# Turning only the maxima's parts, and norming rows a batch sooner

## The chip, the cores and the metric

One core of a Trainium2 chip. PE is TensorE, DVE is VectorE, ACT is ScalarE, POOL is GpSimd, and SP issues most transfers. The metric is the device time of one execution in microseconds; a kernel is told by the median of its runs.

## The reference, cut to what matters

```python
h = _L0_tok_ref(x, ...)                    # 8 x 1024 x 64
h = jnp.concatenate([h, txt], axis=1)      # 8 x 1056 x 64
h = h + _L0_attn_ref(_layernorm(h, axis=-1), qkv_w, qkv_b, proj_w, proj_b, rpb_table)
h = h + _L0_ffn_ref(_layernorm(h, axis=-1), ...)
h = h + _L1_attn_ref(_layernorm(h, axis=-1), ...)
h = h + _L1_ffn_ref(_layernorm(h, axis=-1), ...)
# _L0_attn_ref: 8 heads of 8, 1056 rows
attn = jnp.einsum('bnhd,bmhd->bhnm', q * scale, k)
attn = jax.nn.softmax(attn + bias[None], axis=-1)
out = jnp.einsum('bhnm,bmhd->bnhd', attn, v)
```

The change touches the layer norm ahead of the first attention, and the first attention's scores.

## The kernel before, in words

The kernel is a row of stages, each with its own code on each engine; between stages results go through DRAM, and a stage's buffers lie beside those of its neighbours. The order of work on every engine is written out by hand, with semaphores between them. Two stages are touched.

**heads_prep** ("the preparation", tiles `pre_...`) goes over 8 batches of 1056 rows, 9 tiles of 128 rows. DVE measures mean and variance (`measure`, L717 to L725), POOL takes the root (`root`, L784), DVE norms the rows (`norm`, L730). PE turns the normed rows (`turn`, L824), ACT copies them out (`copy_turned`, L872), PE multiplies them by the query, key and value weights (L831). Each number is then written as a sum of three bf16 parts into rows of 64 slots for each head, queries into `qs` and keys into `ks`: ACT writes the high part three times (L886), DVE forms the rest (L960), POOL writes the queries' middle part (L804) and ACT the keys' (L905), DVE the low part (`low`, L944). Slots 0 to 2 of every head stay empty in the queries and hold ones in the keys. PE turns `qs` and `ks` to 64 slots by rows (L849, 8 groups of 8, through three PSUM banks, and L856 for the last 32 rows), DVE copies the turned queries out (L969, tails L973), ACT the turned keys (L910). SP stores values, the stacked queries `qs` (`qs_d`, L762), turned queries (`qt_d`, L767) and turned keys (`kt_d`, L769). In batch b DVE begins with `measure` and `norm` of batch b + 1, then makes the rests and low parts of b. ACT begins b + 1's high parts only when the store of b's `qs` has landed (`qs_out`). In batch 3, SP issues the next stage's first loads (`ahead`); after batches 4 to 6 DVE makes a part of the next stage's corner (`early`, L1455 to L1465).

**attend_heads** ("the first attention", tiles `att_...`) goes over 32 pairs of heads, one after the other. For the next pair, PE computes all scores once in bf16 (L1531 and others, 37 pieces in three PSUM banks) and DVE takes their maxima over the keys (L1711, L1713, L1716). DVE writes the negated maxima, again as three bf16 parts, into slots 0 to 2 of the stacked queries `qs` that were loaded from `qs_d` (L1723 to L1730); PE turns the whole of `qs` (`turn`, L1552 and L1554), and ACT copies the result to `qm` (`turned`, L1651 and L1654). The scores of the pair are then key times `qm` (L1592, L1595), so that the maxima are subtracted by the matmul; ACT takes the exponential (L1679), and PE multiplies by the values (L1624). The maxima are computed from `qT`, which was loaded from `qt_d` and has empty slots 0 to 2.

What PE does beside each of the 27 pieces of a pair's scores is in one list, in which the turn stands between the third and the fourth maximum of the pair after the next:

```python
AHEAD, BETWEEN = 9, 3
side = ([("max", 1, m) for m in range(AHEAD, NM)] + [("max", 2, m) for m in range(BETWEEN)]
        + [("turn", 1, w) for w in range(QT)] + [("max", 2, m) for m in range(BETWEEN, AHEAD)])
```

Each entry takes the next of three banks (`ring_free`): PE waits until DVE has reduced, or the turned queries have been copied out of, what stood in it three entries earlier. PE waits for both turned parts (`t_cp`) ahead of a pair's first scores.

Of the kernel before, what the change touches and what calls it, by code (L numbers as in the profile page):

```python
# [24 lines left out]
P = 128  # L25
# [620 lines left out]
def heads_prep(nc, a, const, ps, h_in, qt_d, kt_d, qs_d, v_d, vt_d):  # L646
# [9 lines left out]
    with ExitStack() as ctx:  # L656
# [21 lines left out]
         tail_cp, vt_made, q_out, k_out, vt_out, qs_out) = nm.sems(  # L678
            "w_in", "w_scaled", "zeroed", "ones_set", "t_in", "t_split", "consts_set", "st_made", "agg_made",
            "var_made", "tail_set", "half_set", "rstd_made", "xn_made", "xt_mm", "xt_cp", "qkv_mm", "hi_made", "rest_made",  # L680
            "qmid_made", "kmid_made", "low_made", "qt_mm", "qt_cp", "kt_cp", "tail_cp", "vt_made", "q_out", "k_out", "vt_out",
            "qs_out")
# [17 lines left out]
        def ready(sp, b):  # L700
            for x in (q_out, k_out, vt_out, qs_out):
                sp.wait_ge(x, 16 * (b + 1))
            sp.wait_ge(v_out[b % 2], 16 * (b // 2 + 1))
# [42 lines left out]
        def _(sp):  # L746
            enter(sp, const, "sp")
            first_loads(sp, const)

            def step(b, par, more):  # L750
# [20 lines left out]
            two_ahead(sp, step)  # L771

        @block.gpsimd
        def _(pool):
# [20 lines left out]
            tidy(pool, const)  # L795
            for b in range(0, B):
                if b + 1 < B:
                    root(b + 1)
                for m in range(NB):
# [5 lines left out]
                        .then_inc(qmid_made, 1)  # L805
                pool.wait_ge(qmid_made, (b + 1) * NB)
# [57 lines left out]
        def _(act):  # L864
            enter(act, const, "act")
            act.wait_ge(ones_set, 5)
            def copy_turned(b):
                at_least(act, qkv_mm, b * NB)
                for c in range(3):
# [46 lines left out]
        def _(dve):  # L916
# [61 lines left out]
            by_two(dve, step)  # L978
# [372 lines left out]
def attend_heads(nc, a, const, ps, qt_d, kt_d, qs_d, v_d, vt_d, o_d, corner):  # L1351
# [30 lines left out]
    with ExitStack() as ctx:  # L1382
        nm = Names(nc, ctx, const, stage)
        qT = nm.sb("qT", [P, U, N], BF16)
        qm = nm.sb("qm", [P, 2, N], BF16)
        qs = nm.sb("qs", [P, U, NT, P], BF16)
# [14 lines left out]
        (set_up, mrow_set, t_in, cor_rest, cor_hi, s_mm, p_made, pv_mm, o_cp, mx_mm, mx_red, m_row, m_hi, m_r1, m_mid,  # L1401
         c_made, t_mm, t_cp) = nm.sems(
            "set_up", "mrow_set", "t_in", "cor_rest", "cor_hi", "s_mm", "p_made", "pv_mm", "o_cp", "mx_mm", "mx_red", "m_row",
# [4 lines left out]
        NL = 16 * 9  # L1408
# [18 lines left out]
        def load(sp, it, u):  # L1427
# [80 lines left out]
        def _(pe):  # L1508
# [38 lines left out]
            def turn(w, u, pos):  # L1547

                bank = ps[:, 4 + pos % MRING, :].bitcast(BF16)
                if w == 0:  # L1550
                    for t in range(FULL):
                        mm = pe.transpose(bank[:, t * P:(t + 1) * P], qs[:, u, t, :], eye[:, :])  # L1552
                else:
                    mm = pe.transpose(bank[:, 0:2 * TT], qs[0:2 * TT, u, FULL, :], eye[0:2 * TT, 0:2 * TT])  # L1554
# [26 lines left out]
            def scores(it, u, g, last):  # L1581
# [3 lines left out]
                for c, (_, i) in enumerate(parts):  # L1585
# [5 lines left out]
                    if i is None:  # L1591
                        mm = pe.matmul(ps[0:2 * TT, bank, 0:TH], kz[:, u, :], qm[:, u % 2, cols], start=True, stop=not near)  # L1592
# [51 lines left out]
        def _(act):  # L1644
            enter(act, const, "act")
            def turned(k, u, w):

                bank = ps[:, 4 + side.index(("turn", 1, w)) % MRING, :].bitcast(BF16)
                act.wait_ge(t_mm, k * QT + w + 1)
                if w == 0:  # L1650
                    cp = act.activation(qm[:, u % 2, 0:TX], bank[:, :], ACT.Identity)  # L1651
                else:
                    for s in range(2):
                        cp = act.activation(qm[half(s), u % 2, TX:N], bank[half(s), s * TT:(s + 1) * TT], ACT.Identity)  # L1654
                cp.then_inc(t_cp, 1)

            def step(it, last):
# [7 lines left out]
                for u in range(U):  # L1665
                    for g, (t, parts) in enumerate(groups):
                        for c, (_, i) in enumerate(parts):
# [13 lines left out]
                            if not (last and u == U - 1):  # L1681
                                for w in range(QT):
                                    if cut[n % NU] <= side.index(("turn", 1, w)) < cut[n % NU + 1]:
                                        turned(it * U + u + 1, (u + 1) % U, w)
# [7 lines left out]
            for w in range(QT):  # L1692
                turned(0, 0, w)
# [2241 lines left out]
```

## Time and profile before

| | us |
|---|---|
| median of 3 runs | 2805.91 |
| lowest and highest | 2793.22, 2813.04 |
| the profiled execution | 2807.24 |
| its span, first to last instruction | 2805.4 |
| PE, DVE, ACT, POOL busy | 2508.5, 1976.2, 1523.8, 400.7 |
| moved by transfers | 174.09 MB |

The profile comes from one execution. Busy time is the time in which an engine had an instruction under way; an idle time is put down to what ended it. The granted clock is given in tenths of full speed, where 1.00 is 2.4 GHz and 0.50 is 1.2 GHz. Times in the rows count from the first instruction.

### The profile page before, as it was taken

Reading aid. Unit: us, or ns where it says so; the run is one execution under the profiler, and the core shown is the slowest. Engines: PE = TensorE matmul, PEld = TensorE weight load, DVE = VectorE, ACT = ScalarE, POOL = GpSimd, SP = SyncE. Lnnn points to the kernel's source line nnn. Section 1 sums busy time; section 2 is a strip of 40 time slices with the busy share of each in tenths; the row PEclk is TensorE's granted clock in tenths of the full one; section 3 lists DMA queues with packets and bytes.
Section 4 is the critical chain, followed back from the end, with each engine's and each line's share of the span. In section 5 each row is a group of like instructions: output and inputs, shape, how many; then the busy total and the mean of one; then the engine's idle time right before and its main releaser. Section 6 shows DMA issues by size and latency. Waiting matters only on the chain. (4 is left out here: it accounts for less than half of the span.)

```text
span 2805.4 us, 52471 instructions
## 1 busy us (share of the span) xinstructions
PE 2508.5 (89%) x18409; PEld 1100.5 (39%) x18456; DVE 1976.2 (70%) x5061; ACT 1523.8 (54%) x2639; POOL 400.7 (14%) x500
## 2 busy tenths in 40 slices
PE   7877558999999999998699998997679999699999
PEld 3223542333333333333433333565544444433333
DVE  6776668888888888883477776557676765366665
ACT  4323653777777777775244443325656667143443
POOL 1110210000000000003311112122100101411110
PEclk9998667999999999998699999655689999599999
DMA  2001751111111111122500001234441223701100
GB/s 84 16 16 47 252 206 43 33 48 33 48 48 33 49 39 42 48 53 48 108 18 18 18 15 28 56 83 127 156 141 62 82 62 66 149 12 31 31 21 15
DMA packets 272054, 174.09 MB, mean 62 GB/s; under 512 B 225121, under 2 KB 230050, under 8 KB 270546
## 3 DMA queue, kind: packets, MB, share of 16 engines
q1 hardware_dynamic: 258626, 142.45, 18.9%
q0 software_dynamic: 10368, 19.06, 2.2%
q10 hardware_dynamic: 2808, 9.22, 1.5%
q8 instruction: 158, 2.59, 0.4%
q14 instruction: 94, 0.77, 0.1%
HBM read 96.19 MB, written 74.53 MB: 61 GB/s over the span
## 5 line engine op out<-in xcount | busy, mean ns | idle before, releaser
L1711 DVE TENSOR_REDUCE att_mpart<-ps 128x1 f32<-128x512 f32 x1024 | 635.4, 683 | 82.5 <-PE ps L1531 52.5
L1679 ACT ACTIVATE att_p<-ps 128x704 f32<-128x704 f32 x768 | 543.6, 760 | 136.1 <-PE ps L1595 131.4
L1624 PE MATMUL ps<-att_p,att_v 128*9 128x352 f32 x3072 | 300.5, 462 | 0.1
L1531 PE MATMUL ps<-att_kT,att_qT 64*128 64x512 bf16 x1024 | 276.4, 386 | 20.8 <-DMA att_qz<-qt_d 8.5
L1595 PE MATMUL ps<-att_qm,att_kT 64*128 64x352 bf16 x1536 | 251.8, 317 | 10.5 <-ACT att_p L1679 8.2
L1325 DVE TENSOR_REDUCE cau_mpart<-ps 128x1 f32<-128x512 f32 (+5 forms) x384 | 193.0, 551 | 81.2 <-PE ps L1151 68.0
L2462 ACT ACTIVATE mo_act<-ps,mo_b 128x768 f32<-128x768 f32 x176 | 156.3, 901 | 132.2 <-PE ps L2344 128.7
L2615 DVE TENSOR_TENSOR mo_g<-mo_act,ps 128x768 f32<-128x768 f32 x176 | 167.3, 951 | 77.3 <-PE ps L2379 41.2
L1292 ACT ACTIVATE cau_p<-ps 128x704 f32<-128x704 f32 (+6 forms) x272 | 171.6, 660 | 82.3 <-PE ps L1210 49.6
L3014 ACT ACTIVATE mo_act<-ps 128x1024 f32<-128x1024 f32 (+1 forms) x108 | 102.9, 953 | 194.1 <-PE ps L2928 193.9
L1595 PEld LDWEIGHTS ps<-att_qm,att_kT 64*128 64x128 bf16 x1536 | 82.8, 93 | 287.6 <-issue 278.1
L1502 POOL DMA_DIRECT2D o_d<-att_o x128 | 64.1, 507 | 846.0 <-ACT att_o L1662 845.9
L2344 PE MATMUL ps<-mo_x,mo_wf 64*128 64x384 f32 x704 | 162.9, 540 | 0.9 <-issue 0.9
L3125 DVE TENSOR_TENSOR mo_g<-mo_act,ps 128x1024 f32<-128x1024 f32 (+1 forms) x108 | 122.1, 1130 | 50.1 <-PE ps L2940 47.3
L2396 PE MATMUL ps<-mo_g,mo_w 128*64 128x384 f32 x704 | 151.8, 510 | 0.4 <-DVE mo_g L2615 0.4
L1210 PE MATMUL ps<-cau_qT,cau_kT 128*128 128x352 bf16 (+7 forms) x576 | 128.5, 287 | 1.8 <-ACT cau_p L1292 1.5
L1531 PEld LDWEIGHTS ps<-att_kT,att_qT 64*128 64x128 bf16 x1024 | 85.0, 94 | 88.3 <-issue 54.0
L1148 PE MATMUL ps<-cau_kT,cau_qT 128*128 128x384 bf16 (+5 forms) x353 | 105.4, 331 | 14.6 <-ACT cau_qT L1267 7.7
L2940 PE MATMUL ps<-mo_gx,mo_w 64*128 64x512 f32 (+3 forms) x576 | 112.8, 592 | 0.2 <-DVE mo_g L3125 0.2
L600 DVE TENSOR_TENSOR mix_g<-ps,mix_gamT 128x512 f32<-128x512 f32 x128 | 86.1, 686 | 33.2 <-PE ps L404 32.7
L2952 PE MATMUL ps<-mo_g,mo_w 128*64 128x512 f32 (+1 forms) x432 | 108.8, 582 | 0.4 <-DVE mo_g L3125 0.2
L2928 PE MATMUL ps<-mo_x,mo_w 64*128 64x512 f32 (+1 forms) x432 | 108.8, 581 | 0.0
(446 smaller groups left out, 4271.7 us busy)
## 6 DMA issues: line engine op xcount, KB each, us to landing
qs_d<-pre_qs SPq DMA_DIRECT2D x8, 1152.0 KB, 4.5
att_qs<-qs_d SPq DMA_DIRECT2D x32, 288.0 KB, 4.1
qt_d<-pre_qT SPq DMA_DIRECT2D x8, 1056.0 KB, 4.4
kt_d<-pre_kT SPq DMA_DIRECT2D x8, 1056.0 KB, 7.4
att_kT<-kt_d SPq DMA_DIRECT2D x32, 264.0 KB, 2.8
att_qT<-qt_d SPq DMA_DIRECT2D x32, 264.0 KB, 3.1
cqt_d<-cpr_qT SPq DMA_DIRECT2D x8, 1056.0 KB
cau_qT<-cqt_d SPq DMA_DIRECT2D x16, 528.0 KB, 4.0
```

The lines of the kernel that those rows point to most:

```text
L1210: mm = pe.matmul(ps[r0:r0 + kn, at, off:TH], kT[:, u, tile * P:tile * P + kn], qT[:, u, s, q], start=True, stop=m1 <= m0)
L1292: e = act.activation(p[:, n % RING, :, off:TH], ps[:, bank:bank + 2, off:TH], ACT.Exp)
L1325: red = dve.tensor_reduce(mpart[:, j, s, i:i + 1], ps[:, 4 + place, 0:w], AX.X, ALU.max)
L1531: mm = pe.matmul(ps[:, bank, :], qT[half(s), u, j * P:(j + 1) * P], kT[half(s), u, c * BANK:(c + 1) * BANK], start=True, stop=not near)
L1595: mm = pe.matmul(ps[:, bank + s, 0:TH], kT[half(s), u, i * P:(i + 1) * P], qm[half(s), u % 2, cols], start=True, stop=not near)
L1624: mm = pe.matmul(ps[32 * cg:32 * cg + DV, 7, 0:TH], v[:, u, i, s, :], p[:, r, s, :], start=i < 2, stop=i == FULL - 1)
L1679: e = act.activation(p[:, n % PRING, :, :], ps[:, bank:bank + 2, 0:TH], ACT.Exp)
L1711: red = dve.tensor_reduce(mpart[:, j, s, c:c + 1], ps[:, bank, :], AX.X, ALU.max)
L2344: mm = pe.matmul(ps[0:m, bank + s, 0:EN], wf[s * C:(s + 1) * C, w0 + n * P:w0 + n * P + m], x1[s * C:(s + 1) * C, par, :], start=True, sto ...
L2396: mm = pe.matmul(ps[s * C:(s + 1) * C, ACC, 0:EN], w2[0:m, n, :], g[0:m, (par * NH + n) % RING, s, :], start=n == 0 and not relu, stop=n = ...
L2462: act.activation(act1[0:m, r, :, :], ps[0:m, zb:zb + 2, 0:EN], ACT.Relu, bias=b1[0:m, n:n + 1])\
L2615: dve.tensor_tensor(g[0:m, r, :, :], src[0:m, r, :, :], ps[0:m, bank:bank + 2, 0:EN], ALU.mult)\
```

## The change

In the preparation, `qs` is no longer stored, and nobody waits for that store. `measure` and `norm` run a batch sooner: in batch b DVE begins with `measure` of b + 2, and `norm` of b + 2 comes after the fourth copy of turned queries; `root` of b + 2 comes after POOL's middle parts; SP loads the rows of b + 3 in batch b; measure and norm of batch 1 stand ahead of the loop. ACT's three copies of the next batch's turned rows stand between its middle parts instead of before them.

In the first attention, `qs` is neither loaded nor kept. A tile `mz` of two buffers, cleared once by POOL, takes the maxima's parts only; PE turns it as it turned `qs`, and DVE adds the result to the turned queries `qT` in place, behind the first three maxima of the next pair. The scores read `qT` in place of `qm`.

```diff
 # heads_prep, sync: the loads and stores
+            sp.wait_ge(xn_made, NT)
+            load(sp, 2, 0)
...
-                if more:
-                    sp.wait_ge(xn_made, (b + 1) * NT)
-                    load(sp, b + 2, par)
+                if b + 3 < B:
+                    sp.wait_ge(xn_made, (b + 2) * NT)
+                    load(sp, b + 3, 1 - par)
...
-                sp.wait_ge(low_made, (b + 1) * 2 * NB)
-                sp.dma_start(qs_d[bass.ds(b, 1)].rearrange("b p n -> (b p) n"), qs[:, :, :].rearrange("p t n -> p (t n)"))\
-                    .then_inc(qs_out, 16)
 # gpsimd
+            root(1)
             for b in range(0, B):
-                if b + 1 < B:
-                    root(b + 1)
...
+                if b + 2 < B:
+                    root(b + 2)
 # scalar
-                at_least(act, qs_out, b * 16)
...
-                if not last:
-                    copy_turned(b + 1)
                 for m in range(NB):
                     n = tiles(m)
+                    if not last and 1 <= m < 4:
+                        copy_turned(b + 1, (m - 1,))
 # vector
-                if not last:
-                    measure(dve, b + 1, 1 - par)
-                    norm(dve, b + 1, 1 - par)
+                if b + 2 < B:
+                    measure(dve, b + 2, par)
...
                     dve.tensor_copy(qT[:, u, 0:TX], ps[:, (2 * u) % 3, :].bitcast(BF16)).then_inc(qt_cp, 1)
+                    if u == 3 and b + 2 < B:
+                        norm(dve, b + 2, par)
...
+            measure(dve, 1, 1)
+            norm(dve, 1, 1)
 # attend_heads
-        qm = nm.sb("qm", [P, 2, N], BF16)
-        qs = nm.sb("qs", [P, U, NT, P], BF16)
+        mz = nm.sb("mz", [P, 2, NT, P], BF16)
...
-                             (qs[:, u, :, :], qs_d[bi].rearrange("b p (t n) -> (b p) t n", t=NT)[:, :, u * P:(u + 1) * P]),
...
+            pool.memset(mz[:, :, :, :], 0.0).then_inc(mz_set, 1)
...
-                        mm = pe.transpose(bank[:, t * P:(t + 1) * P], qs[:, u, t, :], eye[:, :])
+                        mm = pe.transpose(bank[:, t * P:(t + 1) * P], mz[:, u, t, :], eye[:, :])
...
-                            mm = pe.matmul(ps[:, bank + s, 0:TH], kT[half(s), u, i * P:(i + 1) * P], qm[half(s), u % 2, cols],
+                            mm = pe.matmul(ps[:, bank + s, 0:TH], kT[half(s), u, i * P:(i + 1) * P], qT[half(s), u, cols],
...
+            def turned(k):
+                u = k % U
+                for w in range(QT):
+                    bank = ps[:, 4 + side.index(("turn", 1, w)) % MRING, :].bitcast(BF16)
+                    dve.wait_ge(t_mm, k * QT + w + 1)
+                    if w == 0:
+                        add = dve.tensor_tensor(qT[:, u, 0:TX], qT[:, u, 0:TX], bank[:, :], ALU.add)
+                    else:
+                        for s in range(2):
+                            add = dve.tensor_tensor(qT[half(s), u, TX:N], qT[half(s), u, TX:N],
+                                                    bank[half(s), s * TT:(s + 1) * TT], ALU.add)
+                    add.then_inc(t_cp, 1)
...
                 for m, (kind, s, j, c) in enumerate(maxes):
+                    if m == BETWEEN and k > 0:
+                        turned(k - 1)
```

ACT's `turned`, which copied to `qm`, goes.

## Rows read from the trace of the kernel before

**Rows 1.** Windows: us, then busy us (count) of PE, PEld, DVE, ACT, POOL; PEclk, DMA, GB/s.

```profile
260.00:415.00 155.00, 93.61 (x792) 82.98 (x792) 97.50 (x417) 98.07 (x336) 28.31 (x49) 0.68 0.60 209
456.00:1310.00 854.00, 836.01 (x7684) 285.62 (x7682) 711.66 (x1357) 650.64 (x1052) 62.10 (x124) 1.00 0.16 41
856.00:883.00 27.00, 26.69 (x252) 9.13 (x251) 23.38 (x45) 20.73 (x36) 2.00 (x4) 1.00 0.17 43
```

**Rows 2.** Waits within ten pairs, 600 to 866.3 us: sum, times, longest.

```profile
ACT att_p L1679 <- PE ps L1595: 40.8, 60, 1.3
```

**Rows 3.** Order of time, DVE, around the turn of one pair: start, us.

```profile
800.07 1.88 DVE L1711 TENSOR_REDUCE att_mpart<-ps 128x1 f32<-128x512 f32 x3
802.77 0.69 DVE L1711 TENSOR_REDUCE att_mpart<-ps 128x1 f32<-128x512 f32 x1 [0.83 <-PE ps L1535]
803.95 9.89 DVE L1711 TENSOR_REDUCE att_mpart<-ps 128x1 f32<-128x512 f32 x16 [0.48 <-PE ps L1531]
```

**Rows 4.** Order of time, ACT, the same stretch.

```profile
802.67 0.39 ACT L1654 ACTIVATE att_qm<-ps 64x32 bf16<-64x32 bf16 x2
```

**Rows 5.** Order of time, PE, the same stretch.

```profile
801.55 0.20 PE L1554 MATMUL ps<-eye,att_qs 64*128 64x64 bf16 x1
...
803.54 0.38 PE L1531 MATMUL ps<-att_kT,att_qT 64*128 64x512 bf16 x2
```

**Rows 6.** Order of time, PE, in the preparation, parts of several batches.

```profile
281.81 3.19 PE L831 MATMUL ps<-pre_w,pre_xT 65*128 65x192 f32 x18
...
287.04 2.10 PE L824 MATMUL ps<-eye,pre_xn 128*64 128x128 f32 x9 [2.04 <-DVE pre_xn L730]
...
292.57 1.01 PE L849 MATMUL ps<-eye,pre_qs 128*128 128x128 bf16 x8 [3.43 <-DVE pre_ks L944]
...
333.38 3.19 PE L831 MATMUL ps<-pre_w,pre_xT 65*128 65x192 f32 x18
...
355.97 3.19 PE L831 MATMUL ps<-pre_w,pre_xT 65*128 65x192 f32 x18
...
375.12 3.19 PE L831 MATMUL ps<-pre_w,pre_xT 65*128 65x192 f32 x18
...
395.43 3.19 PE L831 MATMUL ps<-pre_w,pre_xT 65*128 65x192 f32 x18
...
404.40 1.03 PE L849 MATMUL ps<-eye,pre_qs 128*128 128x128 bf16 x8 [5.78 <-DVE pre_ks L944]
...
411.01 0.25 PE L856 MATMUL ps<-eye,pre_ks 32*128 32x32 bf16 x4
```

**Rows 7.** Order of time, DVE, in the preparation, batches 4 and 6.

```profile
336.44 1.24 DVE L717 BATCH_NORM_STATS2 pre_bst<-pre_h 128x6 f32<-128x64 f32 x9 [2.59 <-DMA pre_h<-hidden]
...
379.27 1.23 DVE L717 BATCH_NORM_STATS2 pre_bst<-pre_h 128x6 f32<-128x64 f32 x9
...
383.54 2.10 DVE L730 TENSOR_SCALAR pre_xn<-pre_h,pre_stats,pre_rstd 128x64 f32<-128x64 f32 x9 [1.99 <-POOL pre_rstd L784]
```

**Rows 8.** Order of time, ACT, in the preparation, batches 1, 4 and 7.

```profile
288.34 1.38 ACT L872 ACTIVATE pre_xT<-ps 64x512 f32<-64x512 f32 x3
...
340.23 0.33 ACT L886 ACTIVATE pre_qs<-ps 128x192 bf16<-128x192 f32 x1 [6.29 <-DMA qs_d<-pre_qs]
...
401.95 1.53 ACT L905 ACTIVATE pre_ks<-pre_rest 128x256 bf16<-128x256 f32 x5
```

**Rows 9.** Page, transfers: KB each, us from issue to landing.

```profile
att_qs<-qs_d SPq DMA_DIRECT2D x32, 288.0 KB, 4.1
```

**Rows 10.** Groups by line and form, DVE: busy, mean ns, idle before.

```profile
L1711 DVE TENSOR_REDUCE att_mpart<-ps 128x1 f32<-128x512 f32 x1024 | 635.4, 683 | 82.5 <-PE ps L1531 52.5 <-PE ps L1535 28.4
...
L3125 DVE TENSOR_TENSOR mo_g<-mo_act,ps 128x1024 f32<-128x1024 f32 x96 | 117.0, 1219 | 45.6 <-PE ps L2940 42.8 <-issue 2.2
...
L969 DVE COPY pre_qT<-ps 128x1024 bf16<-128x1024 bf16 x32 | 22.1, 692 | 28.3 <-PE ps L849 28.3
...
L973 DVE COPY pre_qT<-ps 128x128 bf16<-128x128 bf16 x8 | 1.8, 225 | 1.9 <-PE ps L856 1.8
```

More of the change, by code:

```diff
@@ L643, in ln_scale, with heads_prep @@
     dve.reciprocal(rstd[:, 0:n], sq[:, 0:n]).then_inc(rstd_made, 1)
[L646 removed]
+def heads_prep(nc, a, const, ps, h_in, qt_d, kt_d, v_d, vt_d):
     H, D = 8, 8
@@ L700, in ready @@
         def ready(sp, b):
-            for x in (q_out, k_out, vt_out, qs_out):
+            for x in (q_out, k_out, vt_out):
                 sp.wait_ge(x, 16 * (b + 1))
@@ L748, in _, with step @@
             first_loads(sp, const)
-            def step(b, par, more):
+            sp.wait_ge(xn_made, NT)
+            load(sp, 2, 0)
+            def step(b, par):
                 if b == 3:
                     ahead(sp, const)
-                if more:
-                    sp.wait_ge(xn_made, (b + 1) * NT)
-                    load(sp, b + 2, par)
+                if b + 3 < B:
+                    sp.wait_ge(xn_made, (b + 2) * NT)
+                    load(sp, b + 3, 1 - par)
                 sp.wait_ge(hi_made, (b + 1) * NB)
@@ L769, in step @@
                 sp.dma_start(kt_d[bass.ds(b, 1)].rearrange("b u p n -> p (b u) n"), kT[:, :, :]).then_inc(k_out, 16)
-            two_ahead(sp, step)
+            for b in range(B):
+                step(b, b % 2)
         @block.gpsimd
@@ L866, in _, with copy_turned @@
             act.wait_ge(ones_set, 5)
-            def copy_turned(b):
+            def copy_turned(b, chunks=range(3)):
                 at_least(act, qkv_mm, b * NB)
-                for c in range(3):
+                for c in chunks:
                     n = min(4, NT - 4 * c) * P
@@ L976, in step @@
                     early(dve, const, "dve", b - 3)
-            by_two(dve, step)
+            measure(dve, 1, 1)
+            norm(dve, 1, 1)
+            for b in range(B):
+                step(b, b % 2, b == 0, b == B - 1)
         yield ready
@@ L1348, in attend_causal, with attend_heads @@
         yield ready
-def attend_heads(nc, a, const, ps, qt_d, kt_d, qs_d, v_d, vt_d, o_d, corner):
+def attend_heads(nc, a, const, ps, qt_d, kt_d, v_d, vt_d, o_d, corner):
     stage = "att"
@@ L1407, in attend_heads @@
         block = const["block"]
-        NL = 16 * 9
+        NL = 16 * 8
         def half(s):
@@ L1547, in turn @@
             def turn(w, u, pos):
+                u = u % 2
                 bank = ps[:, 4 + pos % MRING, :].bitcast(BF16)
@@ L1551, in turn @@
                     for t in range(FULL):
-                        mm = pe.transpose(bank[:, t * P:(t + 1) * P], qs[:, u, t, :], eye[:, :])
+                        mm = pe.transpose(bank[:, t * P:(t + 1) * P], mz[:, u, t, :], eye[:, :])
                 else:
-                    mm = pe.transpose(bank[:, 0:2 * TT], qs[0:2 * TT, u, FULL, :], eye[0:2 * TT, 0:2 * TT])
+                    mm = pe.transpose(bank[:, 0:2 * TT], mz[0:2 * TT, u, FULL, :], eye[0:2 * TT, 0:2 * TT])
                 mm.then_inc(t_mm, 1)
@@ L1591, in scores @@
                     if i is None:
-                        mm = pe.matmul(ps[0:2 * TT, bank, 0:TH], kz[:, u, :], qm[:, u % 2, cols], start=True, stop=not near)
+                        mm = pe.matmul(ps[0:2 * TT, bank, 0:TH], kz[:, u, :], qT[:, u, cols], start=True, stop=not near)
                     else:
                         for s in range(2):
-                            mm = pe.matmul(ps[:, bank + s, 0:TH], kT[half(s), u, i * P:(i + 1) * P], qm[half(s), u % 2, cols],
+                            mm = pe.matmul(ps[:, bank + s, 0:TH], kT[half(s), u, i * P:(i + 1) * P], qT[half(s), u, cols],
                                            start=True, stop=not near)
@@ L1645, in _ @@
             enter(act, const, "act")
[L1646 to L1655, printed above, removed]
             def step(it, last):
@@ L1680, in step @@
                             e.then_inc(p_made, 1)
[L1681 to L1684, printed above, removed]
                         if pending is not None:
@@ L1690, in step @@
                 out_third(*pending)
-            for w in range(QT):
-                turned(0, 0, w)
             body(act, step)
@@ L1733, in step @@
                 for u in range(U - 1 if last else U):
-                    make(it * U + u + 1, (u + 1) % U)
-            make(0, 0)
+                    make(it * U + u + 1)
+            make(0)
             body(dve, step)
+            turned(IT * U - 1)
         yield ready
@@ L3881, in program @@
             token_mix(nc, a, const, ps, hid[0]),
-            heads_prep(nc, a, const, ps, hid[0], qt_d, kt_d, qs_d, v_d, vt_d),
-            attend_heads(nc, a, const, ps, qt_d, kt_d, qs_d, v_d, vt_d, o_d, a["corner"]),
+            heads_prep(nc, a, const, ps, hid[0], qt_d, kt_d, v_d, vt_d),
+            attend_heads(nc, a, const, ps, qt_d, kt_d, v_d, vt_d, o_d, a["corner"]),
             project(nc, a, const, ps, "prj", 8, 8, o_d, a["L0_attn_proj_w"], a["L0_attn_proj_b"], hid[0], hid[1]),
```

15 lines of the change are left out of this document (7 added, 8 removed).

## The prediction

> **What bounds the kernel now.** I read the windows of the two stages first, then the waits inside each, then the order of time on each engine.
>
> The first attention (456 to 1310 us) holds PE for 836.01 of 854 us at granted clock 1.00, DVE for 711.66 and ACT for 650.64; one of the 32 pairs of heads takes 26.7 us, and in 27 us PE is busy 26.69, DVE 23.38, ACT 20.73 [rows 1]. ACT's largest wait is for PE's scores, 40.8 us in ten pairs [rows 2]. So PE is the bound of the pairs, DVE has 3.2 us to spare in each, and what ACT gets back is worth nothing there.
>
> The preparation (260 to 415 us) has no full engine: PE 93.61, DVE 97.50, ACT 98.07 of 155 us, granted clock 0.68, DMA 0.60 [rows 1]. It is a chain. The batches' first query/key/value matmuls start at 281.81, ..., 333.38, 355.97, 375.12, 395.43, and the last transposes end at 411.26 [rows 6]. A batch is ACT writing the high parts, DVE the rests and the low parts, then PE turning 8 groups while DVE and ACT copy out; PE's bank reuse ties it to these, and the next batch's first matmul follows. What a batch costs is the front (first matmul to first transpose) and the turning. The front is 10.76 us in batch 1 and 8.97 in batch 7, which has no norm ahead of it; the turning 6.46 and 6.86 [rows 6].
>
> **The change, part by part.**
>
> (a) Preparation, norm moved. Before, DVE starts a batch with measure (2.28 us), waits 1.99 for POOL's root, norms in 2.1, and only then makes the rests [rows 7]. After, measure stands there alone, the root is made while DVE works on, and norm comes behind the fourth query copy. The norm is then between that copy and the tail copies: these, and the stores of turned queries and keys queued on SP behind them, come 2.1 us later. PE needs the tail's bank only after 3.2 us of matmuls, so that is covered. Measure alone ends some 4.5 us into the batch (0 at the first matmul, 2.1 norm less 0.2, 0.3 tails, 2.3 measure), while ACT is still writing high parts until 6.52 (401.95 less 395.43 [rows 6, 8]); DVE catches up. The end of the front is then ACT's: 6.52, plus five middle parts 1.53 [rows 8], plus the three copies of the next batch's turned rows, 1.38 [rows 8], which now stand between them, plus one low part and the handover, 0.3: 9.6 us with overlaps. Turning: PE sits still from 5.3 (3.19 matmuls, 2.10 turning of rows [rows 6], now back to back) to 9.6, a gap of 4.3 where it was 3.43 (turning 6.46) and where 5.78 gave 6.86 [rows 6]: I take 6.5.
> - Batches 1 to 3: 51.57 us before (333.38 less 281.81 [rows 6]); 3 x 16.1 = 48.3 after: 3.3 saved. Batch 0, where PE at half clock sets the front: 0.3.
> - Batch 5: the queue on DVE holds a part of the next stage's corner, measure, wait, norm; the wait of 1.99 goes, nothing else. The gap before turning grows to 6.3, turning by some 1.2: 0.7 saved.
> - Batch 6: nothing is left to measure. Wait and measure go, 4.27 us, the gap costs 0.95 back: 3.3 saved.
> - Batch 7 had no norm: 0.
>
> (b) Preparation, stacked queries not stored. ACT waited for that store once, 6.29 us, in batch 4, whose length is 22.59 us against 17.2 of its neighbours [rows 6, 8]; there SP issues the next stage's first loads, and everything behind them (the rows of a later batch, whose landing DVE awaited 2.59 us until 336.44) is late [rows 7]. Two stacked-query loads of ten loads go from that list of SP, but the list starts 2.1 later because the tail copies do, and I take the two as nearly even, 0.2 later. The rows landed 3.1 us into batch 4 (336.44 less 333.38); with batch 3 shorter by 0.9, those for batch 6's measure land 4.2 us into it, measure ends at 6.5, and rests and low parts take 4.1 more (in batch 1 from the norm's end, some 1.5 us after PE's 287.04, to 292.57 [rows 6]): 10.6; turning 6.8 after a long gap: 17.4. Saved 5.2. In the other batches nobody waited for this store, and I count it at nothing.
>
> Sum of the preparation: 3.3 + 0.3 + 0.7 + 3.3 + 5.2 = 12.8 us.
>
> (c) First attention. 32 loads of 288 KB go [rows 9]; PE never waits for them, DMA is at 0.16: nothing. ACT loses its turned copies, which ended at 803.06 in the pair shown [rows 4]. DVE gains, behind the first three maxima of the next pair, one addition over 1024 columns and two over 32. The transposes are there at 801.75 [rows 5], DVE reaches them at 801.95 and now sits idle 0.83 and 0.48 us on either side of the fourth maximum, 1.31 us together [rows 3]. The trace has no addition of two bf16 tensors. Its nearest row by type, source and columns is the copy of 1024 bf16 out of PSUM, 692 ns; the addition with the same columns in f32 takes 1219 ns [rows 10]. The two narrow ones together I take at 0.25, a tail copy's 225 ns and a bit [rows 10]. I take the copy's price, since the type halves it: a maximum over 512 f32 columns of PSUM takes 683 ns, the copy of 1024 bf16 692 [rows 10]. 0.69 + 0.25 = 0.94, inside 1.31. The new wait for the transposes has the fourth maximum and all behind it queued on DVE; PE waits for those through its ring of three banks, and for the additions before it refills the two turned banks and before the next pair's first scores. Then the banks are free at 802.95, earlier than ACT's 803.06, and PE asks for them at 803.54 [rows 4, 5]: 0 per pair. With 1.22 + 0.25 = 1.47 they are free at 803.45: still before 803.54, and DVE is 0.16 late: at most 0.2 x 31 = 6 us. Below nothing: PE pauses 0.3 us in 27 [rows 1], so 31 pairs can't give more than some 5 us, and those pauses are not at the turn.
>
> The Trainium skill speaks on both sides of that price. "VectorE: DVE Perf Modes", section "What auto-detection actually checks", has two elements a cycle for an instruction whose tensors are all 16-bit with unit step, two-source ones included; that would be 0.69. Section "Mode 1× (REGULAR) — the baseline" of the same page counts operands in PSUM among what falls back to one element a cycle; that would be 1.22. The rows of the copy agree with the first for one source; no row has two.
>
> (d) Edges. POOL clears the new tile, 2304 columns, after its last middle part; it has the whole last turning for it, 404.40 to 411.26 [rows 6], before DVE comes to the stage: nothing; were it longer, it would cost its excess once. At the stage's first pair the additions stand where ACT copied: 0 to 0.3 us.
>
> **The sum.** The profiled execution took 2807.24 us, span 2805.4 and 1.8 around it. 2807.2 - 12.8 = 2794.4; the median of the runs shown, 2805.91, is 1.3 lower, so 2793.1: 2793.
>
> **The rivals.**
> 1. Slower: the hole is no hole. DVE idles 0.48 us before the fifth maximum because PE's next maxima stand behind a group of values; if the addition costs 1.22 and PE's order just shifts with it, only the 0.83 is filled, and 1.47 - 0.83 = 0.64 us is added to each of 31 pairs: 20 us, 2813, which is above 2806. It decides once additions and hand-overs pass 1.31 us; below 0.94 it is out. For it: DVE runs 16 maxima without a pause behind this place, at 0.617 each, so a delay is not made good soon, and PE's three banks leave it 0.2 us of room. Against: DVE has another 2 us idle later in the pair, and the type argues for 0.94.
> 2. The moved work comes late: stores and row loads on SP queue 2.1 us later in a stage with DMA at 0.60, where DVE already awaited rows once, and measure, now at the front of DVE's queue, waits for them in several batches. Then only the store's 5.2 us of batch 4 remain and (a) gives 0 to 2: 2800. Against: rows are asked for a whole batch ahead, and 1.15 MB a batch leave the queues.
> 3. Clock: shorter batches keep PE busier and the granted clock, 0.68 now, stays at its upper level through the turning, which would take about half: 3 us in each of 7 batches, 2793 - 21 = 2772. Against: the one long gap of 4.3 us before turning replaces two of 2.0 and 3.43, and after 3.43 the turning already began at the lower level.
> 4. The change doesn't do what it says: ACT and DVE were bound by each other in every batch and only the 6.29 us wait counted; 2800 again, counted with 2.
>
> **From this to the numbers.** Forecast 0.60, rival 1 0.14, rivals 2 and 4 0.13, rival 3 0.08, the rest 0.05 (later stages land on other clock levels; the three runs shown span 20 us). The forecast's own range is 2784 (turning 5.6 instead of 6.5 in six batches, 4 us of PE's pauses) to 2799 (6 us of addition). For 8 in 10 the range takes in rivals 1, 2 and 4 and leaves rival 3 out: 2780 to 2813. A measurement tells about 1% (28 us) from no change. Faster by more: rival 3 and the forecast's lower edge in a low draw, 0.12. Slower by more needs 1.3 us in every pair: 0.05. Within: 0.83.
>
> **What the profile would show.** Additions of 128x1024 bf16 at 0.7 us (or 1.2), DVE idle before the fourth and fifth maximum gone, PE without waits for DVE, the pair still at 26.7 us. In the preparation: batches of some 16.1 us, batch 4 near 17.4, batch 6 near 17, no wait of ACT for a store, POOL's root not waited for from batch 0 on, first attention's first score 12 to 13 us earlier. I am wrong if the pair moves by over 0.2 us, if measure waits for its rows, or if the turning changes its level.

## The result, and the profile after

The changed kernel took 2784.9 us in the median of 14 runs (2773.72 to 2792.5), the kernel before 2800.5 in 14 runs; the ratio is 0.9943, 95% interval 0.9928 to 0.9957: 16 us (0.6%) faster, with 1.0 outside the interval. The profiled execution took 2779.05 us, its span 2777.3.

Two groups of the page, from the first attention. The maxima on DVE stand behind 55.6 us of idle time (82.5 in [rows 10]); ACT waits longer for PE's scores, 208.0 us in all where it was 131.4, now that it has no turned queries to copy.

```profile
L1714 DVE TENSOR_REDUCE att_mpart<-ps 128x1 f32<-128x512 f32 x1024 | 633.9, 684 | 55.6 <-PE ps L1534 50.5
L1672 ACT ACTIVATE att_p<-ps 128x704 f32<-128x704 f32 x768 | 546.5, 760 | 215.0 <-PE ps L1599 208.0
```

Windows of the changed kernel, as [rows 1]:

```profile
260.00:415.00 155.00, 91.91 (x805) 83.44 (x805) 103.28 (x426) 98.33 (x336) 30.84 (x53) 0.72 0.49 163
440.00:1292.00 852.00, 837.20 (x7679) 287.19 (x7679) 738.30 (x1453) 616.02 (x958) 62.33 (x124) 1.00 0.12 31
856.00:883.00 27.00, 26.10 (x243) 9.06 (x235) 23.55 (x47) 18.92 (x31) 2.00 (x4) 1.00 0.12 32
```

In the first attention PE is as busy as before (837.20 of 852 us), DVE has 738.30 where it had 711.66, ACT 616.02 for 650.64; transfers fell from 0.16 to 0.12. In the preparation the granted clock went from 0.68 to 0.72 and transfers from 0.60 to 0.49 in the window shown; over the stage alone the clock is 0.68 before and 0.75 after.

The order of time on PE in the preparation, beside [rows 6]:

```profile
282.65 3.19 PE L831 MATMUL ps<-pre_w,pre_xT 65*128 65x192 f32 x18
...
285.68 1.15 PE L824 MATMUL ps<-eye,pre_xn 128*64 128x128 f32 x9
...
292.48 1.01 PE L849 MATMUL ps<-eye,pre_qs 128*128 128x128 bf16 x8 [5.66 <-DVE pre_ks L943]
...
332.29 3.19 PE L831 MATMUL ps<-pre_w,pre_xT 65*128 65x192 f32 x18
...
342.15 1.01 PE L849 MATMUL ps<-eye,pre_qs 128*128 128x128 bf16 x8 [5.68 <-DVE pre_ks L943]
...
347.87 3.19 PE L831 MATMUL ps<-pre_w,pre_xT 65*128 65x192 f32 x18
...
359.19 1.01 PE L849 MATMUL ps<-eye,pre_qs 128*128 128x128 bf16 x8 [7.15 <-DVE pre_ks L943]
...
364.92 3.19 PE L831 MATMUL ps<-pre_w,pre_xT 65*128 65x192 f32 x18
...
381.31 3.19 PE L831 MATMUL ps<-pre_w,pre_xT 65*128 65x192 f32 x18
...
396.89 0.25 PE L856 MATMUL ps<-eye,pre_ks 32*128 32x32 bf16 x4
```

The stage starts at 265.82 and its last transposes end at 397.14: 131.32 us, where before had 147.05 (264.21 to 411.26). PE turns the normed rows at once behind its 3.19 us of matmuls, in 1.15 us at granted clock 1.00, where before it stood still for 2.04 us and then took 2.10 at 0.50. Fronts (first matmul to first transpose) and turnings of each batch, read off such rows, in us:

```
batch                  0      1      2      3      4      5      6      7    sum
front, before      11.00  10.76  11.13  10.76  15.83  13.53  14.53   8.97
front, after       10.85   9.83   9.85   9.85   9.86  11.32  10.10   8.97
turning, before     6.60   6.46   6.21   6.25   6.76   5.62   5.78   6.86
turning, after      5.98   6.58   6.77   6.76   5.72   5.73   6.29   6.86
saved, forecast      0.3          3.3            5.2    0.7    3.3      0   12.8
saved, measured      0.8          1.9            7.0    2.1    3.9      0   15.7
```

DVE at the end of batch 3: norm, the tail copies, then measure, which waited 0.17 us for its rows where [rows 7] had 2.59.

```profile
332.24 2.09 DVE L729 TENSOR_SCALAR pre_xn<-pre_h,pre_stats,pre_rstd 128x64 f32<-128x64 f32 x9
334.24 0.22 DVE L973 COPY pre_qT<-ps 128x128 bf16<-128x128 bf16 x1
334.37 0.22 DVE L973 COPY pre_kT<-ps 128x128 bf16<-128x128 bf16 x1
334.76 1.24 DVE L716 BATCH_NORM_STATS2 pre_bst<-pre_h 128x6 f32<-128x64 f32 x9 [0.17 <-DMA pre_h<-hidden]
```

ACT in batch 2, beside [rows 8]: the copies stand between the middle parts, and the last middle part begins at 307.76. The batch's first matmul stands at 299.06 and the transposes start at 308.91.

```profile
305.58 0.42 ACT L904 ACTIVATE pre_ks<-pre_rest 128x256 bf16<-128x256 f32 x1
306.02 0.59 ACT L872 ACTIVATE pre_xT<-ps 64x512 f32<-64x512 f32 x1
306.51 0.40 ACT L904 ACTIVATE pre_ks<-pre_rest 128x256 bf16<-128x256 f32 x1
306.82 0.58 ACT L872 ACTIVATE pre_xT<-ps 64x512 f32<-64x512 f32 x1
307.30 0.41 ACT L904 ACTIVATE pre_ks<-pre_rest 128x256 bf16<-128x256 f32 x1
307.60 0.26 ACT L872 ACTIVATE pre_xT<-ps 64x128 f32<-64x128 f32 x1
307.76 0.61 ACT L904 ACTIVATE pre_ks<-pre_rest 128x256 bf16<-128x256 f32 x2
```

The turn of one pair on DVE, beside [rows 3]. The addition takes 0.68, the two narrow ones 0.35. The idle 0.83 us is filled; of the 0.48 ahead of the fifth maximum 0.43 is left: the fourth maximum starts 2.77 us after the first where it was 2.70, the fifth 3.89 where it was 3.88.

```profile
785.18 1.88 DVE L1714 TENSOR_REDUCE att_mpart<-ps 128x1 f32<-128x512 f32 x3
786.98 0.68 DVE L1696 TENSOR_TENSOR att_qT<-att_qT,ps 128x1024 bf16<-128x1024 bf16 x1
787.58 0.35 DVE L1699 TENSOR_TENSOR att_qT<-att_qT,ps 64x32 bf16<-64x32 bf16 x2
787.95 0.69 DVE L1714 TENSOR_REDUCE att_mpart<-ps 128x1 f32<-128x512 f32 x1
789.07 9.85 DVE L1714 TENSOR_REDUCE att_mpart<-ps 128x1 f32<-128x512 f32 x16 [0.43 <-PE ps L1534]
```

And on PE, beside [rows 5]: the additions are done at 787.93, PE refills the banks from 788.66.

```profile
786.67 0.20 PE L1558 MATMUL ps<-eye,att_mz 64*128 64x64 bf16 x1
...
788.66 0.38 PE L1534 MATMUL ps<-att_kT,att_qT 64*128 64x512 bf16 x2
```

From one pair's turn to the next it is 26.61 us (26.64 before), and 27.39 (27.43) at every fourth; from the first turn to the last 830.92 us, 832.69 before.

So 15.7 us come from the preparation and 1.8 from the pairs; the profiled executions differ by 28.2. Of the rest 9.0 us are in a stage that the change doesn't touch, the one that writes `lin_qf`. Its windows, of the kernel before and of the changed one:

```profile
1745.00:1862.10 117.10, 108.70 (x440) 67.17 (x439) 66.57 (x308) 42.89 (x116) 19.91 (x17) 0.59 0.21 50
```

```profile
1728.50:1836.60 108.10, 91.68 (x429) 58.70 (x429) 66.16 (x308) 42.62 (x116) 19.93 (x17) 0.68 0.23 54
```

It is the same work at a granted clock of 0.59 and of 0.68. Both windows begin 10 us ahead of the stage, which took 107.1 and 98.1 us; the last section comes back to it.

### The profile page after: what moved, and what is told of

Its sections match the earlier page's. It is cut to its first block and busy times, and to the rows that moved or that the text cites. A ratio compares the mean times of both kernels' runs of the same rounds, so it can differ in the third digit from the quotient of the medians.

```text
span 2777.3 us, 52433 instructions
## 1 busy us (share of the span) xinstructions
PE 2486.6 (90%) x18409; PEld 1091.5 (39%) x18456; DVE 2000.7 (72%) x5157; ACT 1489.1 (54%) x2543; POOL 402.9 (15%) x501
## 3 DMA queue, kind: packets, MB, share of 16 engines
q8 instruction: 158, 2.59, 0.4%
## 5 line engine op out<-in xcount | busy, mean ns | idle before, releaser
L1714 DVE TENSOR_REDUCE att_mpart<-ps 128x1 f32<-128x512 f32 x1024 | 633.9, 684 | 55.6 <-PE ps L1534 50.5
L1672 ACT ACTIVATE att_p<-ps 128x704 f32<-128x704 f32 x768 | 546.5, 760 | 215.0 <-PE ps L1599 208.0
L1599 PE MATMUL ps<-att_qT,att_kT 64*128 64x352 bf16 x1536 | 251.5, 317 | 7.3 <-ACT att_p L1672 6.9
L1599 PEld LDWEIGHTS ps<-att_qT,att_kT 64*128 64x128 bf16 x1536 | 82.1, 93 | 272.7 <-issue 262.8
```

The source lines that it names most:

```text
L1672: e = act.activation(p[:, n % PRING, :, :], ps[:, bank:bank + 2, 0:TH], ACT.Exp)
L1714: red = dve.tensor_reduce(mpart[:, j, s, c:c + 1], ps[:, bank, :], AX.X, ALU.max)
```

## The experiments

Each kernel was built from the changed one unless its text says otherwise. The stage is measured from the first query/key/value matmul to the end of the last transposes, and pairs by the median from turn to turn, in each one's profiled execution; ratios are to the kernel before, run beside it, and where the interval takes in 1.0 the time shows no gain.

```
kernel              stage us   pair us   median us   ratio, 95% interval
before                147.05     26.64
changed               131.32     26.61     2784.90   0.9943, 0.9928 to 0.9957
changed, again        132.73     26.60     2789.39   0.9952, 0.9931 to 0.9973
norm alone            138.51     26.65     2796.32   0.9989, 0.9970 to 1.0007
turn alone            143.27     26.61     2796.08   0.9983, 0.9963 to 1.0003
store kept            136.17     26.61     2791.04   0.9960, 0.9940 to 0.9980
add and copy          131.25     26.79     2782.82   0.9941, 0.9920 to 0.9961
copies first          133.18     26.61     2788.89   0.9948, 0.9926 to 0.9970
norm behind tail      131.78     26.60     2775.63   0.9915, 0.9883 to 0.9946
corner later          129.44     26.60     2775.98   0.9915, 0.9884 to 0.9945
corner later, again   129.51     26.61     2782.03   0.9931, 0.9904 to 0.9958
20 matmuls            131.57     26.61     2775.37   0.9915, 0.9884 to 0.9946
5 and 8 matmuls       124.81     26.60     2779.27   0.9917, 0.9886 to 0.9948
5 and 8 or 16         121.47     26.61     2768.59   0.9885, 0.9855 to 0.9915
```

Medians of four to fourteen runs move by 4 to 6 us for the same kernel (2784.90 and 2789.39; 2775.98 and 2782.03), and the changed one, the norm behind the tail and the 20 matmuls, whose stages are within 0.5 us of each other, have medians up to 9.5 us apart. So the steps between these kernels are read from the stage and the pairs, and not from the medians.

**Norm alone.** The kernel before with the new schedule of the preparation; the store, its wait, the loads and ACT's copies stay.

```diff
-                    measure(dve, b + 1, 1 - par)
-                    norm(dve, b + 1, 1 - par)
+                    measure(dve, b + 2, par)
...
+                    if u == 3 and b + 2 < B:
+                        norm(dve, b + 2, par)
```

> The kernel before with only the schedule of the preparation changed (measure and norm a batch sooner, ACT's turned copies between its middle parts); the stacked queries are stored, awaited and loaded, and ACT copies the turned ones. From the first query/key/value matmul of the preparation to its last transposes the kernel before takes 147.05 us, the changed one 131.32. If the norm and the store each do their own part, this one keeps batch 4's wait for the store, some 6 us, and has all the rest: 137.5 us, pairs at 26.64, a time 9 to 10 us under before (ratio 0.9966). If only the wait for the store had counted: 145 to 147 us and no gain.

It was 138.51 us, 1 us over my sum: the fronts are within 0.25 us of the changed kernel's but for batch 4's, 17.82 us, longer than before's 15.83. The time gained less than I expected, ratio 0.9989 for 0.9966, and its interval takes in 1.0, so only the stage shows the gain. ACT's wait for the store is 8.47 us there, against 6.29 in [rows 8]:

```profile
341.13 0.33 ACT L891 ACTIVATE pre_qs<-ps 128x192 bf16<-128x192 f32 x1 [8.47 <-DMA qs_d<-pre_qs]
```

**Turn alone.** The changed kernel with the preparation's schedule as before.

```diff
-                if b + 2 < B:
-                    measure(dve, b + 2, par)
+                if not last:
+                    measure(dve, b + 1, 1 - par)
+                    norm(dve, b + 1, 1 - par)
```

> The changed kernel with the preparation's schedule put back as before: no store, no load of stacked queries, DVE adds in the first attention. If the norm does most: 143 us from the first matmul to the last transposes (batch 4 gives 4 of its 5, since DVE still has measure, wait, norm ahead of the rests), pairs at 26.61 to 26.64, 4 to 5 us under before (0.9983). If the store and its traffic do most: 135 us and 12 us under before.

It was 143.27 us. Only batch 4's front differs from before's by over 0.2 us: 11.03 instead of 15.83. The norm does most. Here too the interval of the ratio takes in 1.0. The parts alone save 8.5 and 3.8 us of the stage, together 15.7, and the 3.4 us between lie in batch 4's front: the norm moved alone makes it 2.0 longer, since SP then issues the store 4.4 us into the batch for 2.1 and ACT waits longer for it; leaving the store out alone makes it 4.8 shorter, and both together 6.0.

**Store kept.** The store and ACT's wait put back, the loads not.

```diff
+                sp.wait_ge(low_made, (b + 1) * 2 * NB)
+                sp.dma_start(qs_d[...], qs[:, :, :]...).then_inc(qs_out, 16)
...
+                at_least(act, qs_out, b * 16)
```

> The changed kernel with the store of the stacked queries and ACT's wait for it put back, but not the loads. If batch 4 waits because SP reaches that store late: SP's list of first loads is now shorter, ACT waits some 3.4 us once, 134.7 us from the first matmul to the last transposes, 3.4 us over the changed kernel. If the traffic of the stores matters (1.15 MB a batch), other batches grow too and the rows of batch 6 come late: over 137 us.

It was 136.17 us, 4.85 over the changed kernel, all of it in batch 4: front 14.81 for 9.86, ACT's wait 5.26. I had expected 3.4: the transfer took longer than I gave it, issued at 330.14 it released ACT at 335.57.

```profile
330.14 0.63 SPq L763 DMA_DIRECT2D qs_d<-pre_qs  x1
...
335.57 0.33 ACT L889 ACTIVATE pre_qs<-ps 128x192 bf16<-128x192 f32 x1 [5.26 <-DMA qs_d<-pre_qs]
```

The fronts of batches 1, 2, 3, 5 and 6 are 9.85, 9.85, 9.86, 10.97 and 9.86, no more than 0.02 us longer than without it: 1.15 MB more a batch delay nobody there.

**Add and copy.** One more copy of 1024 columns ahead of each addition.

```diff
                     if w == 0:
+                        dve.tensor_copy(spare[:, :], bank[:, :])
                         add = dve.tensor_tensor(qT[:, u, 0:TX], ...)
```

> The changed kernel with one more copy of 1024 columns by DVE ahead of each addition, 0.6 us per pair, so that some 1.6 us stand where the holes of 0.83 and 0.48 us were. If both holes take it and PE is the bound: 26.6 to 26.8 us per pair, 0 to 5 us over the changed kernel. If only the first hole can be filled (my first rival): 0.6 to 0.75 more in every pair, 27.3, 20 us over the changed kernel.

26.79 us a pair, 0.18 more, 5.6 us from the first turn to the last (the medians, 2782.82 and 2784.90, don't show it). DVE, the same stretch:

```profile
784.53 1.88 DVE L1716 TENSOR_REDUCE att_mpart<-ps 128x1 f32<-128x512 f32 x3
786.33 0.68 DVE L1697 COPY att_spare<-ps 128x1024 bf16<-128x1024 bf16 x1
786.93 0.68 DVE L1698 TENSOR_TENSOR att_qT<-att_qT,ps 128x1024 bf16<-128x1024 bf16 x1
787.52 0.35 DVE L1701 TENSOR_TENSOR att_qT<-att_qT,ps 64x32 bf16<-64x32 bf16 x2
787.90 10.55 DVE L1716 TENSOR_REDUCE att_mpart<-ps 128x1 f32<-128x512 f32 x17
```

The copy and the additions fill 1.57 us without a pause before or behind, so both holes take work. What is left over shows as a new wait of PE, ten times in ten pairs:

```profile
PE ps L1535 <- DVE att_mpart L1716: 2.0, 10, 0.2
```

My first rival had 0.64 us a pair at a price of 1.47 us; at 1.57 it is 0.18, so it is refuted.

**Copies first.** ACT's three turned copies ahead of its middle parts again.

```diff
+                if not last:
+                    copy_turned(b + 1)
                 for m in range(NB):
-                    if not last and 1 <= m < 4:
-                        copy_turned(b + 1, (m - 1,))
```

> The changed kernel with ACT's three copies of the next batch's turned rows ahead of its middle parts again. If ACT's middle parts end the front, as I summed, it doesn't matter where the copies stand for the last middle part: 9.85 us of front as now, 131.3 us in all. If the low parts on DVE end it, which want the middle parts one by one: the first comes 1.2 us later, DVE can't start, 2.0 us of low parts follow from there, and the front grows by 0.3 to 1 us in six batches: 133 to 137 us.

Fronts of 9.99 to 10.02 us in batches 1 to 4, 0.16 more than with the copies between: that is between my sum's 0 and the rival's 0.3, so DVE's wait for the middle parts counts, but for less than the rival had. The other 1 us of the 133.18 is in turnings (6.76, 6.58, 6.76 in batches 4 to 6 for 5.72, 5.73, 6.29), and such turnings also differ between two executions of the changed kernel. That part of the change is worth 0.16 us a batch in those batches.

**Norm behind the tail copies.**

```diff
-                    if u == 3 and b + 2 < B:
-                        norm(dve, b + 2, par)
...
                                     ...then_inc(tail_cp, 1)
+                if b + 2 < B:
+                    norm(dve, b + 2, par)
```

> The changed kernel with the norm behind the tail copies. If the place between is only a cover, as I said: the stores go out 2.1 us sooner, nobody waited for them, 131.3 us and the time as changed. If SP's later queue cost something in batch 4 or 5: up to 1 us less. If DVE then stands in the way at the tail, up to 0.3 us a batch more, because it waits for PE's last transposes before it can norm: 133 us.

131.78 us, fronts the same but for 0.14 more in batches 5 and 6. So it matters little where the norm stands, as summed.

**Corner parts later**, run twice.

```diff
-                if b in (4, 5, 6):
-                    early(dve, const, "dve", b - 3)
+                if b in (5, 6, 7):
+                    early(dve, const, "dve", b - 4)
```

> The changed kernel with the three corner parts of the next stage after batches 5, 6 and 7, not 4, 5 and 6. Batch 5's front is 11.3 us now because a corner part, measure and norm queue on DVE; it should fall to 9.85, and the part behind batch 7 lie in the 8.5 us in which PE waits for the first attention's loads: 129.8 to 130 us, and the first score matmul 1.4 us sooner. Rival: DVE ends that last part later than the loads land, and the gap of 8.5 us grows.

> The kernel with the corner parts behind batches 5, 6 and 7 once more, beside the one above: 129.4 us in the preparation, as before, and a time some 2 us under the changed kernel, ratio 0.9935 to before, since its 0.9915 came from four runs.

129.44 and 129.51 us; batch 5's front fell from 11.32 to 9.86. But the first score matmul came 9.96 and 9.95 us behind the last transposes, where before and the changed kernel have 8.49 and 8.48:

```profile
392.65 0.25 PE L856 MATMUL ps<-eye,pre_ks 32*128 32x32 bf16 x4
402.86 0.58 PE L1534 MATMUL ps<-att_kT,att_qT 64*128 64x512 bf16 x1 [9.96 <-DMA att_qz<-qt_d]
```

So 1.5 of 1.9 us went back. DVE was done with the corner at 396.99, so it isn't the rival. Nor is it SP's list: SP issued the first two `att_qz` loads 3.95 us behind the last transposes, and 3.97 in the changed kernel, but PE was released 6.0 us after that for 4.5, so the load took longer to land. The two kernels below, with the same corner, have 8.49 and 8.47. Turn alone has 9.34, the others 8.4 to 8.5. Why the load took longer stays open.

**Matmuls of unused results**, to test the third rival. They leave the work as it is and add matmuls whose results nobody reads. First 20 a batch:

```diff
                 if not last:
                     turn(b + 1)
-                    pe.wait_ge(xt_cp, b * 3 + 6)
+                pe.wait_ge(rest_made, b * 2 * NB + 2)
+                for _ in range(20):
+                    pe.matmul(ps[:, 3, 384:512], const["eye"][:, :], const["eye"][:, :], start=True, stop=True)
+                if not last:
+                    pe.wait_ge(xt_cp, b * 3 + 6)
```

> The changed kernel with 20 matmuls of 128 f32 columns on PE in every batch, between the turning of rows and the first transposes, into columns of a bank whose rests are made; their results are not used. If the sum's term for the turning is a term of the clock (my third rival): granted clock near 1.00 from there on, turning in 4.6 to 5.2 us where ACT's copies of 1.02 us bind, instead of 5.7 to 6.8, 8 to 12 us less, 120 to 123 us. If the turning is bound by the copies anyway: under 2 us less; and if the 20 matmuls outlast the front, each batch grows.

The turnings came out as expected, 4.78 to 5.06 us in all batches, at granted clock 1.00 in batch 4's. So did the other end, fronts of 13.67, 14.29, 13.62 and 12.34 in batches 0, 4, 5 and 6, and with them the stage took 131.57 us and not 120 to 123. In batch 4:

```profile
333.96 7.55 PE L838 MATMUL ps<-eye 128*128 128x128 f32 x40 [2.72 <-DVE pre_rest L962]
```

PE waited 2.72 us for the first rests, then took 7.55 for the 20, which the trace records as 40. Then 5 ahead of the turning of rows and 8 behind, with the corner later:

```diff
+                if not first:
+                    pe.wait_ge(tail_cp, b * 2)
+                    pe.wait_ge(kt_cp, b * 4)
+                    for _ in range(5):
+                        pe.matmul(ps[:, 2, 384:512], const["eye"][:, :], const["eye"][:, :], start=True, stop=True)
                 if not last:
                     turn(b + 1)
-                    pe.wait_ge(xt_cp, b * 3 + 6)
+                if not first:
+                    pe.wait_ge(rest_made, b * 2 * NB + 2)
+                    for _ in range(8):
+                        pe.matmul(ps[:, 3, 384:512], const["eye"][:, :], const["eye"][:, :], start=True, stop=True)
+                if not last:
+                    pe.wait_ge(xt_cp, b * 3 + 6)
```

> The changed kernel with the corner parts a batch later (as in the kernel with them behind batches 5 to 7) and with fewer matmuls of unused results: 5 between the query/key/value matmuls and the turning of rows, 8 behind it, none in batch 0. The run with 20 had turnings of 4.8 to 5.1 us but fronts of up to 14.3, because its matmuls started only when DVE had made the first rests and outlasted the front. If that is all that stood against it: fronts 9.86 in batches 1 to 6, 9.0 in batch 7, turnings near 5.0, 120 us from the first matmul to the last transposes, 11 us under the changed kernel and ratio 0.990 to before. If 13 matmuls are too few for the upper clock level, turnings stay at 5.7 to 6.8 and it is 129 us, like the kernel with the corner parts moved alone.

124.81 us and not 120: fronts as expected but batch 4's 10.81, where measure waited 2.54 us for its rows, and turnings 4.77, 4.78, 5.95, 5.15, 5.71, 5.90, 5.92 in batches 1 to 7. PE stood still for 2.75, 2.78 and 2.77 us ahead of the first three; all three began with 8 transposes in 0.61 us, and in the third they went on with 8 in 1.06. So with such a gap the lower level comes back in some batches and not in others. With 16 instead of 8 in batches 1, 2, 3 and 5:

```diff
+                n2 = 16 if b in (1, 2, 3, 5) else 8
...
-                    for _ in range(8):
+                    for _ in range(n2):
```

> As the kernel with 5 and 8 matmuls of unused results, with 16 in place of the 8 in batches 1, 2, 3 and 5, where the gap of 2.75 us that was left ahead of the turning lets them. In the run with 8, turnings of 4.8 stood beside some of 5.9 and the stage took 124.8 us. If the gap left is what brings the lower clock back in some batches: 4.8 to 5.0 in batches 2 to 4 and 6, 121 to 122 us. If the level falls for another reason (a budget over the stage): no change, 124 to 125 us.

121.47 us, turnings 4.77, 5.48, 5.30, 4.77, 4.78, 5.69 and 4.87 in batches 1 to 7, granted clock 0.92 in the stage. PE in batch 3, with 0.99 us left idle ahead of the transposes at 322.77:

```profile
312.92 3.19 PE L831 MATMUL ps<-pre_w,pre_xT 65*128 65x192 f32 x18
315.95 1.28 PE L838 MATMUL ps<-eye 128*128 128x128 f32 x10
317.06 1.15 PE L824 MATMUL ps<-eye,pre_xn 128*64 128x128 f32 x9
318.05 3.74 PE L845 MATMUL ps<-eye 128*128 128x128 f32 x32
322.77 0.61 PE L860 MATMUL ps<-eye,pre_qs 128*128 128x128 bf16 x8 [0.99 <-DVE pre_ks L954]
```

```profile
265.30:386.90 121.60, 102.84 (x1031) 96.32 (x1029) 90.42 (x390) 96.78 (x335) 29.93 (x50) 0.92 0.52 176
```

In batches 2 and 3, expected at 4.8 to 5.0, all transposes ran at the upper level, 8 in 0.61 us. What made these turnings longer is that ACT waited for the store of the last batch's turned keys before its first copy, 2.40 us in batch 2:

```profile
309.29 1.94 ACT L920 ACTIVATE pre_kT<-ps 128x1024 bf16<-128x1024 bf16 x2 [2.40 <-DMA kt_d<-pre_kT]
```

Ratio 0.9885, interval 0.9855 to 0.9915, 32 us under before; the whole interval lies under the changed kernel's 0.9928 to 0.9957. Against before the stage gives 25.6 of the 32 us.

**The changed kernel again.**

> The changed kernel itself, beside the one above on the same chip: 131.3 us in the preparation, pairs at 26.61, ratio 0.994. Of the stages behind, which no kernel here touches, it tells how far they move by themselves: the stage with lin_qf took 107.1 us in the profiled execution of before and 98.1 in that of the changed kernel, and I expect one of these two values and not one between.

132.73 us and not 131.3: batch 4's front is 11.13 for 9.86, since measure waited 2.50 us for its rows in this execution.

```profile
336.27 1.23 DVE L716 BATCH_NORM_STATS2 pre_bst<-pre_h 128x6 f32<-128x64 f32 x9 [2.50 <-DMA pre_h<-hidden]
```

The untouched stage took 107.7 us. In the 14 profiled executions of all kernels it took 107 to 108 nine times, 98 three times and 100 twice, so nearly, but not quite, one of two values. Its window in this execution, which also begins 10 us ahead of the stage:

```profile
1728.20:1845.90 117.70, 109.76 (x441) 68.02 (x439) 66.66 (x309) 43.06 (x116) 19.91 (x17) 0.57 0.21 49
```

## Why the prediction was right

- The bound: PE in the pairs, a chain in the preparation. Right: 1.0 us more on DVE and the turned copies gone from ACT moved a pair by 0.03 us.
- (a) Fronts of 9.6 in batches 1 to 3 were 9.83 to 9.85; the turning, put at 6.5, was 6.58 to 6.77. Both a little over: 1.9 saved for 3.3. The front's shape was right: high parts until 6.52 as summed, ACT's middle parts and copies 2.79 (summed as 1.53 and 1.38), and 0.54 for the last low part and the handover, which I had put at 0.3. The gap ahead of the turning was 5.7 and not 4.3, since I kept 2.10 us for the turning of rows, which took 1.15. In batches 5 and 6 I charged the longer gap with 1.2 and 0.95 us of slower turning; it cost 0.1 and 0.5, so they saved 2.1 for 0.7 and 3.9 for 3.3. The mis-sized term is that a longer gap means a longer turning: 5.72 to 6.86 stood behind gaps of 5.66 to 7.15 us in no order.
- (b) Batch 4 saved 7.0 for 5.2, and 5.0 of it is the store, by the kernel that kept it. I had the rows landing 4.2 us into the batch; in this execution DVE waited 0.17 us for them, in another 2.50, when batch 4 took 16.97: between 5.6 and 7.0. That wait of 2.50 us is one of the three signs by which I said I would be wrong; it came in batch 4 alone, where the sum had it. The kernel that kept the store shows that it cost nothing outside batch 4.
- (c) The addition cost 0.68 as the copy did, and nobody waited for it. It needed the first hole only: 0.43 us stayed idle ahead of the fifth maximum, where I had said that both would go. The row of 1219 ns that I took for an addition in f32 is a product (`mo_g`, L3125), so the f32 price of an addition is in no row. The Trainium skill, "VectorE: DVE Perf Modes", section "What auto-detection actually checks", has the mode 2×_1P if every tensor is 16-bit with unit step, and the median of 678 ns for 1024 columns agrees. The Trainium skill's section "Mode 1× (REGULAR) — the baseline" of the same page says that operands in PSUM work in the one-element mode; my reading, that one such operand forces it, doesn't hold here.
- (d) POOL's clearing took 2.02 us from 389.6 on, and DVE first wrote to the tile at 435.2; the first pair cost nothing (35.7 us from the first matmul of the maxima to the first score, before and after).
- Rival 1 is refuted by the added copy. Rival 2 occurred in batch 4 only, as a wait of up to 2.5 us, worth some 1.3. Rival 3 didn't happen by itself (granted clock 0.68 to 0.72, and every turning began with 8 transposes in 1.01 to 1.04 us); its price, 3 us a batch and 21 in all, was twice too high: with the level held up a turning took 4.8 for 5.7 to 6.9, and the stage lost another 8 to 10 us. Rival 4 is refuted by the norm alone: with the wait for the store still there, the stage lost 8.5 us.
- Against its own execution my sum was 2794.4 and the time 2779.05: 2.9 us are in the preparation, 1.8 in the pairs, most of the rest in the stage with `lin_qf`, whose clock differed. The medians, 2800.5 to 2784.9, moved by 15.6, what the two touched stages give together (17.5) within 2 us. The forecast of 2793 is some 8 us over the 2784.9: 5.4 of them because I started from 2805.91, the median of three runs, where 14 runs had 2800.5, and 2.8 by the sum, 12.8 for 15.6. That the sum came so close is in part luck: its terms miss by 1.4 us one way and by 4.3 the other.

## What to carry to other kernels

Work that makes the next link of a chain wait belongs a step earlier, behind the last thing that others wait for; here that gave more (8.5 us) than the transfers that were left out with it (3.8). When two edits touch the same queue, run each alone and both together: here they gave 15.7 together. An idle hole can be filled only if the engine that releases its end doesn't wait for the filler: compare the time at which the filler is done with the time at which it is asked for.

## What the runs showed of the hardware

- With PE idle 5.7 to 7.2 us ahead of them, in batches 1 to 7 of the changed kernel, the transposes start at the lower of the two clock levels, 1.2 GHz (granted clock 0.50, 8 of them in 1.01 us), and the whole turning takes 5.7 to 6.9 us. In batch 3 of the last kernel, with 0.99 us of idle, they run at the upper level (1.00, 8 in 0.61 us). The windows show the start of batch 1's turning in the one and of batch 3's in the other:

```profile
292.40:294.40 2.00, 1.92 (x19) 1.95 (x20) 0.69 (x1) 0.00 (x0) 0.00 (x0) 0.50 1.04 298
```

```profile
322.70:324.70 2.00, 1.93 (x32) 1.80 (x32) 1.08 (x2) 0.26 (x1) 0.00 (x0) 1.00 0.47 155
```

- At the upper level a turning takes 4.8 us, and ACT's four copies of 1.02 us then follow each other with 0.19 us of idle between them (20 matmuls, batch 4). Filling only a part of the gap (5 and 8 matmuls, 2.2 to 2.8 us left in six of seven batches) wasn't enough everywhere: 4.8 to 6.0 us.
- DVE adds two bf16 tensors, one of them in PSUM, in 678 ns for 1024 columns; the product of two f32 tensors, one of them in PSUM, took 1219 for as many.
- A stage that nobody touched (the one with `lin_qf`) took 98.1 us in one execution of the changed kernel and 107.7 in another, in windows with granted clocks of 0.68 and 0.57. That is 9.6 of the 12.8 us by which these two executions differ (2779.05 and 2791.87). Why the clock differs stays open.
